# A four-layer graph network on one core: step tiles of the last step on ScalarE alone, first head's sums in the aggregation banks, and a new order of casts, masks and products in the first step

## The reference

```python
x = _layernorm(x + _L0_gnn_ref(x, adj, Wq, bq, Wk, Wv, bv))   # attention, masked by the 0/1 adjacency
x = _layernorm(x + _L1_gnn_ref(x, adj, W, b))    # adj / row sum @ x @ W.T + b, leaky relu
x = _layernorm(x + _L2_gnn_ref(x, adj, W, a))    # four heads: softmax over sources of leaky(s_i + s_j)
x = _layernorm(x + _L3_gnn_ref(x, adj, B))       # symmetric normalised adj with an added diagonal @ x @ B
```

## Time and profile before

| | us |
|---|---|
| median of 3 runs | 891.36 (889.5 to 893.33) |
| the profiled execution itself | 891.38 |
| its span in the profile | 889.6 |
| PE busy | 826.2 (93%) |
| DVE busy | 711.1 (80%) |
| ACT busy | 613.7 (69%) |
| POOL busy | 300.1 (34%) |
| chain that ended last | PE 79%, DVE 12%, ACT 3%, issue 3% |

### The profile page before, as it was taken

One profiled execution on the slowest core, in us unless ns is written; L12 is line 12 of the kernel. 1 busy time (PEld: TensorE's weight loads), 2 busy tenths in 40 slices (PEclk: granted clock), 3 DMA queues, 4 the chain that ended last, 5 costly groups with the idle time before them and its releaser, 6 DMA issues.

```text
span 889.6 us, 25379 instructions
## 1 busy us (share of the span) xinstructions
PE 826.2 (93%) x10856; PEld 679.5 (76%) x10856; DVE 711.1 (80%) x1651; ACT 613.7 (69%) x732; POOL 300.1 (34%) x311
## 2 busy tenths in 40 slices
PE   5987999999999999999999999999999999983885
PEld 3576689857997589967998579976898579972884
DVE  3436777988979887988979888897979889786984
ACT  2574586787859775896758777697868878566641
POOL 2022432326413442326413362235223263134501
PEclk9898999999999999999999999999999999996897
DMA  9905116480377415491375603692264902930100
GB/s 180 157 25 95 49 49 103 71 175 13 97 98 125 114 49 92 66 180 48 96 99 97 141 12 98 86 171 68 72 92 87 182 2 73 134 59 25 58 18 24
DMA packets 166464, 77.40 MB, mean 87 GB/s; under 512 B 136624, under 2 KB 154160, under 8 KB 166352
## 3 DMA queue, kind: packets, MB, share of 16 engines
q1 hardware_dynamic: 156864, 58.48, 33.9%
q0 software_dynamic: 8448, 16.78, 10.7%
q10 hardware_dynamic: 1040, 0.52, 0.2%
HBM read 54.66 MB, written 4.33 MB: 66 GB/s over the span
## 4 chain that ended last, share of the span: by engine, by line
PE 79%; DVE 12%; issue 3%; ACT 3%; POOL 0%; POOLq 0%; DVEq 0%
PE ring L1301 20%; PE ring L1247 13%; PE Z L1269 12%; PE Z L1318 12%; PE ring L1282 9%; PE ring L1245 3%; PE ring L1334 2%; PE ring L1183 2%; DVE ring L793 2%; PE ring L1212 2%; DVE cmat L848 2%; PE ring L1167 1%; DVE x L884 1%; DVE x L981 1%; DVE meanvar L877 1%
## 5 line engine op out<-in xcount | busy, mean ns | idle before, releaser
L666 ACT ACTIVATE steps<-sjrow,steepsi 128x1024 bf16<-128x1024 f32 x248 | 266.3, 1138 | 96.3 <-DVE cmat L848 74.4
L848 DVE TENSOR_TENSOR cmat<-steps,adj 128x1024 f16<-128x1024 bf16 x180 | 153.8, 899 | 34.7 <-PE ring L1301 21.8
L1301 PE MATMUL ring<-vparts,cmat 128*128 128x66 bf16 x4416 | 145.0, 194 | 17.3 <-DVE vparts L996 7.7
L1301 PEld LDWEIGHTS ring<-vparts,cmat 128*128 128x128 f16 x4416 | 142.4, 98 | 18.9 <-issue 8.6
L1269 PEld LDWEIGHTS Z<-vv,probs 128*128 128x128 f32 x1024 | 123.1, 192 | 21.4 <-issue 17.2
L1247 PE MATMUL ring<-qT,xT 128*128 128x512 f32 x256 | 139.5, 627 | 0.0
L1269 PE MATMUL Z<-vv,probs 128*128 128x129 f32 x1024 | 123.4, 275 | 0.0
L682 ACT ACTIVATE probs<-ring 128x1024 f32<-128x1024 f32 x64 | 65.4, 1021 | 70.6 <-PE ring L1247 69.7
L490 POOL TENSOR_SCALAR vareps<-meanvar 128x4 f32<-128x4 f32 x64 | 13.6, 212 | 281.5 <-DVE meanvar L877 281.5
L1282 PE MATMUL ring<-vparts,adj 128*128 128x132 bf16 x1536 | 94.0, 222 | 0.0
L1282 PEld LDWEIGHTS ring<-vparts,adj 128*128 128x128 f16 x1536 | 93.3, 96 | 0.1
(11 more groups left out here) (131 smaller groups left out, 1334.8 us busy)
## 6 DMA issues: line engine op xcount, KB each, us to landing
adj<-in_adj_dram POOLq DMA_DIRECT2D x16, 1024.0 KB, 12.9
sjrow<-sj_rows SPq DMA_DIRECT2D x31, 512.0 KB, 4.0
out_dram<-x SPq DMA_DIRECT2D x16, 256.0 KB, 2.4
x<-in_x_dram SPq DMA_DIRECT2D x7, 512.0 KB, 4.2
adjT<-adj SPq DMA_TRANSPOSE x64, 3.4
cmat<-adj SPq DMA_TRANSPOSE x56, 4.5
x<-in_x_dram ACTq DMA_DIRECT2D x1, 512.0 KB, 4.3
small<-in_a_dram SPq DMA_DIRECT2D x1, 128.0 KB, 11.3
```

The source lines that it names most:

```text
L666: act.activation(steps[:, n % STEPS, :], sjrow[:, h % 2, :], ACT.Relu, bias=steepsi[:, t, h:h + 1], scale=STEEP).then_inc(step_made, 1)
L848: dve.tensor_tensor(c_of[:, t, :], steps[:, n % STEPS, :], adjs[o.parity][:, t, :], ALU.min)\
L1301: last = pe.matmul(s[:, jt, 0:VW], c_of[:, t, jt * P:(jt + 1) * P], vparts[:, t, h, part, :], start=t == 0 and part == 0, stop=t == T - 1 ...
```

## The change

In the last step, all 32 tiles go the way of step tile and minimum; the comparison is gone from the program, and with it `minussi`. `sjb` moves from Z into a ring slot of its own, and head 0's sums move from a ring slot into Z, so the third aggregation now waits until head 0 has been combined. `turn_largest` comes before the product of `sj` on TensorE, and ScalarE copies `sjb`, makes the first step tile, makes the factors, and only then copies `sj`. POOL adds the diagonal only after `x2` is normalised.

In the first step, DVE casts `q` before the first four masks; the first score tile starts with its two products and adds the masks after them; ScalarE makes tile 3 of the next graph's masks after `xT` and not before the widening; and DVE casts the next graph's `x` and `q` behind the two halves of layer 1's output, not ahead of the first half and behind the first normalisation.

```diff
-            seq += of(n - 1, ("wh", 0), ("wh", 1), ("sj", 0))
+            seq += of(n - 1, ("wh", 0), ("wh", 1), ("sjb", 0), ("sj", 0))
...
-        seq += of(n - 1, *(masks + c if n < NB else c[:1] + masks + c[1:]))
+        seq += of(n - 1, *(masks + (c if n < NB else c[1:])))
...
-    STEP_TILES = {"full": every_tile, "last": [(h, t) for h, t in every_tile if t % 4 != 3]}
+    STEP_TILES = {"full": every_tile, "last": every_tile}
...
+        def slot_of_head(kind, o, h):
+
+            return Z if kind == "last" and h == 0 else slot("c", o, h)
...
                 if kind == "last":
+                    pool.wait_ge(normed[1], o.count(2, 2))
                     add_diagonal(kind, o)
...
                     for name, k, tiles in (("x2T", 0, [4]), ("wh", 0, []), ("wh", 1, [5]), ("sj", 0, [6, 7])):
+                        if kind == "last" and name == "sj":
+                            act.wait_ge(sjb_full, 1)
+                            act.activation(sjrow[:, 0, :], whole(slot("sjb", o, 0)), ACT.Copy).then_inc(sjb_read, 1)
+                            step_tile(kind, o, 0)
+                            factors(o)
                         take_group(kind, o, name, k)
...
-                            else:
+                            elif n < 7:
                                 make_maskb(Graph(1), [n - 4])
...
-                        make_maskb(following, ([4], [5], [6, 7])[n])
+                        make_maskb(following, ([3, 4], [5], [6, 7])[n])
...
-                    if (h, t) in STEP_TILES[kind]:
-                        n = STEP_TILES[kind].index((h, t))
-                        dve.wait_ge(step_made, o.count(H * T, n + 1))
-                        dve.tensor_tensor(c_of[:, t, :], steps[:, n % STEPS, :], adjs[o.parity][:, t, :], ALU.min)\
-                            .then_inc(c_made, 1)
-                    else:
...
-                        dve.scalar_tensor_tensor(c_of[:, t, :], sjrow[:, h % 2, :], minussi[:, t, h:h + 1],
-                                                 adjs[o.parity][:, t, :], ALU.is_ge, ALU.mult).then_inc(c_made, 1)
+                    n = STEP_TILES[kind].index((h, t))
+                    dve.wait_ge(step_made, o.count(H * T, n + 1))
+                    dve.tensor_tensor(c_of[:, t, :], steps[:, n % STEPS, :], adjs[o.parity][:, t, :], ALU.min)\
+                        .then_inc(c_made, 1)
...
                     cast_x(g)
+                    cast_q(g)
                     make_first_maskb(0)
-                    cast_q(g)
...
-                if more:
+                if kind == "full" and more:
                     cast_x(following)
                 for k in range(2):
                     layer1_out(kind, g, k)
                     norm_stats(1, g, x2, k)
+                    if kind == "first":
+                        (cast_x, cast_q)[k](following)
...
-                if more:
+                if kind == "full" and more:
                     cast_q(following)
...
+                if first:
+                    pe.wait_ge(dve_init, 1)
+                    for j in range(2):
+                        product(j, True, False)
+                for j in range(2):
+                    if first:
+                        last = mask(j, False, True)
+                    else:
+                        mask(j, True, False)
+                        last = product(j, False, True)
...
                 if kind == "last":
-                    pe.wait_ge(mall_read, o.count(1, 1))
+                    pe.wait_ge(read["c"], o.count(2 * H, 2))
                 aggregate(o, "agg3", "out3", parts3, (split3, o.count(6, 6)), agg3T, b3_s,
...
-                    for name, k in (("x2T", 0), ("wh", 0), ("wh", 1), ("sj", 0)):
+                    for name, k in (("x2T", 0), ("wh", 0), ("wh", 1)):
                         head_inputs(kind, o, name, k)
+                    head_zero_inputs(o)
+                    turn_largest(kind, o)
+                    head_inputs(kind, o, "sj", 0)
+                    spread_largest(kind, o)
```

More of the change, by code:

```diff
@@ L661, in step_tile @@
                     act.wait_ge(c_made, o.count(H * T, was_h * T + was_t + 1))
+                if n == 0:
+                    act.wait_ge(steepsi_made, o.count(1, 1))
                 if t == 0 and h in ROWS[kind]:
@@ L693, in step @@
                             make_maskb(g, tiles)
-                made = 0
+                made = 1 if kind == "last" else 0
                 if kind != "last":
@@ L926, in combine @@
                 n = outs(h, k)
-                sums = by_tile(slot("c", o, h))[:, ts, :]
+                sums = by_tile(slot_of_head(kind, o, h))[:, ts, :]
                 if n == 0:
@@ L1144, in claim @@
                     was, of, j = SEQ[n - SLOTS]
-                    if was == "out3":
+                    if was == "sjb":
+                        pe.wait_ge(sjb_read, 1)
+                    elif was == "out3":
                         pe.wait_ge(y_made[3], Graph(of).count(2, j + 1))
@@ L1201, in head_inputs @@
                 else:
[L1202 to L1208, removed]
                     s = claim("sj", o, 0)
@@ L1214, in head_inputs, with head_zero_inputs @@
                     last.then_inc(full["sj"], 1)
-            def turn_largest(kind, o):
[L1218 to L1223, removed]
+            def head_zero_inputs(o):
+                sjb = claim("sjb", o, 0)
+                for c in range(2):
+                    last = pe.matmul(sjb[:, c, :], wext[:, D + H:D + H + 1].broadcast_to([P, P]),
+                                     x2T[:, c * 512:(c + 1) * 512], start=True, stop=True)
+                last.then_inc(sjb_full, 1)
+            def turn_largest(kind, o):
+                pe.wait_ge(read["x2T"], o.count(1, 1))
                 pe.wait_ge(mloc_made, o.count(1, 1))
@@ L1237, in scores, with mask @@
                 s = claim("st", g, n)
-                for j in range(2):
+                first = kind == "first" and n == 0
+                def mask(j, start, stop):
                     kt = 2 * (n % 4) + j
-                    if kind == "first" and n == 0 and j == 0:
-                        pe.wait_ge(dve_init, 1)
                     if n % 4 == 0 and j == 0:
@@ L1244, in scores, with product @@
                     for q in range(4):
-                        pe.matmul(s[:, j, q * P:(q + 1) * P], maskb[:, 4 * c + q, kt * P:(kt + 1) * P],
-                                  ident16[:, :], start=q == 0, stop=False, skip_group_check=True)
-                    last = pe.matmul(s[:, j, :], xT[:, kt * P:(kt + 1) * P], qT[:, c * 512:(c + 1) * 512],
-                                     start=False, stop=True, skip_group_check=True)
+                        last = pe.matmul(s[:, j, q * P:(q + 1) * P], maskb[:, 4 * c + q, kt * P:(kt + 1) * P],
+                                         ident16[:, :], start=start and q == 0, stop=stop, skip_group_check=True)
+                    return last
+                def product(j, start, stop):
+                    kt = 2 * (n % 4) + j
+                    return pe.matmul(s[:, j, :], xT[:, kt * P:(kt + 1) * P], qT[:, c * 512:(c + 1) * 512],
+                                     start=start, stop=stop, skip_group_check=True)
+                if first:
[8 more added lines that the diff above has]
+                        last = product(j, False, True)
                 last.then_inc(full["st"], 1)
@@ L1289, in head_sums @@
                 c_of = (C_OF if kind == "full" else C_LAST)[h]
-                s = by_tile(claim("c", o, h))
+                if kind == "last" and h == 0:
+                    pe.wait_ge(mall_read, o.count(1, 1))
+                else:
+                    claim("c", o, h)
+                s = by_tile(slot_of_head(kind, o, h))
                 for jt in range(T):
@@ L1391, in step @@
                 if kind == "last":
-                    turn_largest(kind, o)
-                    spread_largest(kind, o)
                     head_sums(kind, g, 0)
```

16 lines of the change are left out of this document (2 added, 14 removed).

## The result

The changed kernel takes 875.24 us in the median of 6 runs (874.16 to 877.05), the kernel before 891.19 in the median of 6 (889.5 to 893.33): 16.0 us less, a ratio of 0.9824 (95%: 0.9806 to 0.9842). The forecast was 877.4.

What follows compares the result with a forecast made beforehand. TensorE holds four fifths of the chain, so only its stops and low-clock stretches matter. Terms 3.7 + 2.7 + 1.7 + 2.5 + 1.7 + 1.7 = 14.0 off 891.38 give 877.4; bounds 875.8 to 886.1, own range 875 to 881, wider range 873 to 886.

Steps and rivals of the forecast that it cites:

- First step: First step up to the first aggregation: second score tile starts at 25.2 against 28.96, 3.7 us less (2.0 to 3.9).
- the term's low end: First step: 2.0 us gained if thinner work leaves the clock low when the second score tile runs, losing some 1.7.
- the mask taken from before the widening: First step, ScalarE's queue: moving this mask of about 1 us counted as nothing, at most 0.15 us.
- Seam: First to second step: the second step's first score tile comes 2.7 us earlier, between 1.0 and 3.3.
- A fall of the clock in the gap: First to second step: could cut the gain of 2.7 us to its low end, 1.0.
- The middle: Seven full steps: one small DVE operation less in each, beside TensorE's work, gains nothing.
- Normalisation: Entry of the last step: with POOL's diagonal addition behind it, normalisation takes 1.10 and not 2.78 us, 1.7 less.
- Clock at the last entry: Last step's transposes and `wh`: clock stays at the upper level with the longer wait gone, 2.5 us less, else 0.
- the first rival: Last entry: the clock falls all the same, the 2.5 us go, total 879.9; chance 0.17.
- Head 0: Last step: 1.2 us from two tiles made by minimum, 0.5 from the earlier first step tile; 1.7, between 0.6 and 2.5.
- Head 1: Last step: head 1 no longer waits for head 0's combination to free its slot, 1.7 us less, 0 if tiles late.
- ScalarE as the bound: Last step's heads: rival that ScalarE's step tiles alternate with DVE's minima and set the pace, 903 us; chance 0.04.

Runs made afterwards that it cites:

- act_more: The changed kernel with three more ScalarE activations, 3.03 us into tiles nobody reads, ahead of the last four step tiles: 876.52 us.
- diag_early: The changed kernel without POOL's wait for the normalisation, so the diagonal is added as early as before: 879.6 us.
- first_alone: The kernel before with only the first step's edits (casts, first score tile, mask tile 3): 884.43 us.
- casts_back: The changed kernel with the next graph's casts of `x` and `q` back in their old places on DVE: 877.49 us.
- wait_head0: The changed kernel with TensorE made to wait, before head 1's sums, until DVE has read head 0's: 877.68 us.

## Why the prediction was right, step by step

The mechanisms came as forecast and in the places named. The measured 875.24 is 2.2 us under the 877.4 forecast, at the lower edge of the forecast's own 875 to 881 and below 875.8, the sum of all large ends. The terms as measured below come to 15.3 against the 14.0 taken: all but the normalisation came out a little larger than they were put. The other 0.7 belongs to no term: 0.4 lies in stretch E, and 0.3 in C, where head 0's last pass (7.99 before) takes anything from 6.8 to 8.1. That part is luck, of the kind for which the prediction allowed some 2 us either way.

- **First step, 3.7.** 3.75 in the changed kernel's trace; in the ten traces of stretch A the second tile starts between 24.7 and 25.5, in the median at 25.0, which makes it 3.9. At which level the products run (3.53 here, 1.98 in act_more, diag_early and first_alone) hardly matters, since TensorE waits for row maximum 4 before the second tile in any case, 1.02 here and 1.49 in act_more and first_alone. In act_more the second tile itself ran at the lower level, the case of the term's low end, and A is 1.4 longer. That the mask taken from before the widening gives nothing on the path is right: the late half of the aggregation starts at 62.66, behind DVE's split and not behind ScalarE, and 37.45 after the second tile, where it was 37.43.
- **Seam, 2.7.** 3.1 in the changed kernel: 2.3 from the order of the casts, by casts_back, and 0.8 with the guard scores no longer at the lower level. Only the first was in the working. A fall of the clock in the gap was the fear, and the gain went the other way.
- **The middle, nothing.** Right: B scatters over 2.3 us and the kernel before lies in the middle of it. The changed kernel's own trace alone has 0.7 more there, which tells nothing.
- **Normalisation, 1.7.** 1.67, and diag_early takes it away again. `layer3_out` ran beside POOL's addition without being slowed (2.15).
- **Clock at the last entry, 2.5.** Right in eight traces of nine: 0.60 in the transposes, 1.83 in `wh` and 0.25 in the product behind it, 2.7. In the ninth the first rival came half true, and that one is the execution profiled: it has 1.7 less of the gain (1.41 in `wh`, 0.31 behind it), about the distance of its 877.05 to the median. One in nine does not speak against the chance of 0.17.
- **Head 0, 1.7.** 2.0 from `sjb` to the last pass: 1.13 from the two tiles, where 1.2 was taken, and 0.9 from what comes before them, where 0.5 was. That 0.9 is read from the rows alone; no run takes the new order of `turn_largest` and the first step tile back.
- **Head 1, 1.7.** 1.9, and wait_head0 takes 1.8 of it back. first_alone shows a price that was not in the term: behind this wait the clock can fall, for another 1.5.
- **ScalarE as the bound.** The rival on the other side did not come. Its cover was put at 3 to 4 us; 3.03 more cost nothing, and 1.37 idle remained. The working took that cover from the time between the last tile on DVE and head 3, and this came out smaller, at 2.5.

## What to carry to other kernels

Look for the engine that idles just ahead of a queue which holds the chain: both gains of the first step are work moved, without being made less, into time in which an engine waited anyway. Where a stretch can run at either level of the clock, one trace shows only one of them, so measure the same stretch in every trace at hand before taking a fall as the rule or building a remedy for it. Matmuls that only hold the clock must be queued ahead of the semaphore wait that they are to fill; behind it they took 5.87 us here and gave back 1.5 to 2.9.

## What the hardware showed that was not expected

With the same instructions and waits of at most 0.8, 0.5 and 1.2 us between them, TensorE's granted clock at the last entry stayed at 1.00 in eight traces and fell to 0.50, which is 1.2 GHz, for three microseconds in one. Head 1 kept the upper level behind waits of 1.65 and 1.69 us and lost it behind one of 1.96. What decides it within such a stretch these rows don't show.
